# BitLinear feed-forward on one core: left blocks of a pair made two pairs ahead, both int8 roundings of a pair on ScalarE

## The chip, the cores and the metric

One core of one Trainium2 chip runs the whole program. The metric is device time in microseconds (us) for one execution, the median of three runs. The core's engines are TensorE (PE in the rows; PEld is its weight load), VectorE (DVE), ScalarE (ACT), GpSimd (POOL) and SyncE (SP), whose queue issues nearly all DMAs here.

## The reference

8192 tokens (128 x 64) of 256 values go through a conditioned RMS norm, a gated up-projection to 2 x 1024, an exact GELU gate, an int8-style rounding per token, and a down-projection with ternary weights:

```python
scale = cond @ norm_w.T + 1.0
h = x * (scale[:, None, :] * rsqrt(mean(x * x, -1) + 1e-6))
val, gate = split(h @ up_w.T)                 # 256 -> 2 x 1024
h = val * gelu(gate)                          # exact
hq = round(h * 127 / max|h|) * max|h| / 127   # per token
y = hq @ ternary(down_w).T + x                # 1024 -> 256
```

## The kernel before

**Tiles.** Tokens are taken in 64 groups of 128 (`G` = 64), four groups to a tile of x (`NG` = 4). A group's left matrix is h: 128 tokens by 256, and its product with the up weights is made in two chunks (`NJ`) of 512 columns, each with a gate and a value half. fp32 operands are split into a high and a low fp16 part and multiplied as hi x hi, hi x lo, lo x hi.

**Pairs.** Groups 12 to 55 (`W0` to `W1`) run as 22 pairs (`NP`). For a pair, chunk 0 is multiplied group by group (`project`), and chunk 1 by a scheme with seven block products instead of eight, for which sums and differences of the pair's left blocks and of weight blocks are needed. So a pair has two left tiles, each turned (transposed) by one DMA into `hpT`: part 0, the own blocks, and part 1, the sums. `hpT` and `hp_hl` have two buffers each. The way of a left tile is: VectorE multiplies x by its scales (`scale_h` into `hp`, line 821, one instruction for each group); GpSimd makes the four sums (`pair_sums`, lines 409 to 414); ScalarE casts to the high part (`pair_high`, line 568); GpSimd subtracts for the low part (`pair_low`, line 418); SP issues the transposing DMA (`turn_pair`, line 299), which must also wait until TensorE is done with that buffer, two pairs back.

**TensorE's order in a pair** (`pair`, products of three matmuls at lines 1097 to 1099, projections of six at 1084 to 1089): the first chain product; gate of the first group; the down-projection of an older group (`downs`, eight matmuls, line 1221); the second chain product, the first that reads part 1; value of the first group; a product into another bank; the third chain product; a product into the bank `ps_two`; gate of the second group; the fourth chain product; value of the second group; the down-projection of another older group; the last product into `ps_two`. The chain accumulates in one bank, and ScalarE copies it out between its products (`pair_copy` 0, 1, 2; lines 575 and 579): the second chain product waits for copy 0, the third for copy 1, the fourth for copy 2.

**Rounding.** For each group VectorE reduces the maximum over 1024 columns, clips it, inverts it and makes the dequantising scale (`token_scale`, `dequant_scale`, lines 878 to 889). In a pair, the earlier group is rounded to int16 on VectorE (line 901) and cast to bf16 there (906); the other is scaled by `trec127` (line 1023), rounded on ScalarE at the end of its pair (`pair_quantise`, line 601) and cast on VectorE (898). SP turns the bf16 tile (`turn_q`, line 307, into `qT`), TensorE multiplies it (`down`), ScalarE scales the result (`scale_y`, line 626), GpSimd adds x (`sum_y`, line 455), and SP stores four groups at once (312) and loads a later tile of x (269). `quantised(g)` says how many groups are rounded by the step of group g: two fewer than g in the pairs.

**Order.** Each engine's order is written out by hand and an engine takes its instructions in that order; a wait on a semaphore holds everything behind it on that engine's queue. In pair i, whose first group is g = 12 + 2i: VectorE begins with `scale_h` of pair i+1, then finishes pair i-1 (`pair_first`: `pair_add` at line 860, the product at 869), then rounds. GpSimd makes the sums and low parts of pair i+1. SP turns part 0 of pair i+1, turns an older q, stores and loads, turns part 1 of pair i+1, and turns the next q.

Of the kernel before, what the change touches and what calls it, by code (L numbers as in the profile page):

```python
# [5 lines left out]
def cond_bitlinear_ffn(nc: bass.Bass, x, cond_norm, up_wT, down_wT, out):  # L6
# [75 lines left out]
    with ctx:  # L82
# [73 lines left out]
        trec127 = sb("trec127", [P, 1], fp32)  # L156
# [104 lines left out]
        def _(sp):  # L261
# [68 lines left out]
            def loads(g):  # L330
                t, n = g // NG, g % NG
                if n == 2 and t + 2 < NT:
# [50 lines left out]
        def _(pool):  # L383
# [97 lines left out]
            for g in range(F32G, W0):  # L481
                if g + AHEAD < W0:
                    low_part(g + AHEAD)
                elif g + AHEAD == W0:
                    pair_sums(0)
                    pair_low(0, 0)
                else:
                    pair_low(0, 1)
                sum_downed(g)
                next_rms(g)  # L490
                if 4 <= g < 8:
                    weight_sum(g - 4)
                if 7 <= g < 11:
                    weight_sum_low(g - 7)
            for i in range(NP):
                g = W0 + 2 * i
                if i >= 1:
                    pair_second(i - 1)
                if i + 1 < NP:
                    pair_sums(i + 1)  # L500
                    pair_low(i + 1, 0)
                    pair_low(i + 1, 1)
                else:
                    low_part(W1)
                    low_part(W1 + 1)
                sum_downed(g)
                next_rms(g + 1)
                sum_downed(g + 1)
            pair_second(NP - 1)
            for g in range(W1, G + 2):  # L510
# [3 lines left out]
                next_rms(g)  # L514

        @block.scalar
        def _(act):
# [143 lines left out]
            for g in range(F32G, W0):  # L661
# [3 lines left out]
                else:  # L665
                    pair_high(0, g + AHEAD - W0)
# [14 lines left out]
                if g % NG < 2:  # L681
                    squares(g // NG + 1, 2 * (g % NG))
                gelu(NJ * g)
            gelu(NJ * W0 - 1)
            for i in range(NP):
# [4 lines left out]
                if i + 1 < NP:  # L690
                    pair_high(i + 1, 0)
                else:
                    high_part(W1)
                pair_copy(i, 1)
                if i + 1 < NP:
                    pair_high(i + 1, 1)
                else:
                    high_part(W1 + 1)
                pair_gelu(i, 1)
                pair_copy(i, 2)  # L700
                if i == 0:
                    squares(g // NG + 1, 0)
                if g % NG == 0:
                    squares(g // NG + 1, 2)
                else:
                    squares(g // NG + 2, 0)
                pair_gelu(i, 2)
                pair_gelu(i, 3)
                scale_downed(g + 1)
                for n in range(quantised(g), quantised(g + 1)):  # L710
                    pair_quantise(n)
            for g in range(W1, G + 2):
# [5 lines left out]
                if g % NG == 1 or (g % NG == 0 and g > W1):  # L718
                    squares(g // NG + 1, 2 * (g % NG))
# [4 lines left out]
        def _(dve):  # L724
# [266 lines left out]

            for g in range(F32G, W0):
                if g + AHEAD < W0:
                    scale_h(g + AHEAD)
                elif g + AHEAD == W0:
                    scale_h(W0)
                    scale_h(W0 + 1)
# [9 lines left out]
            for i in range(NP):  # L1007
                g = W0 + 2 * i
                scale_h(g + 2)
                scale_h(g + 3)  # L1010
                if i >= 1:
                    pair_first(i - 1)
                quantise_step(g)
                pair_first_chunk(i, 0)
                pair_add(i, 1)
                late = range(quantised(g), quantised(g + 1))
                for n in late:
                    token_scale(n)
                    dequant_scale(n)
                    dve.wait_ge(trec_ready, n + 1)  # L1020
                    if n >= W0:
                        dve.wait_ge(qint_ready, n - 1)
                    nc.vector.tensor_scalar(trec127[:, :], trec[:, n % 2:n % 2 + 1], 127.0, None, ALU.mult)\
                        .then_inc(trec127_ready, 1)
                pair_first_chunk(i, 1)
                for n in late:
                    quantise(n, there=True)
            pair_first(NP - 1)
            for g in range(W1, G):
# [275 lines left out]
```

## Time and profile before

| what | us |
|---|---|
| median of 3 runs | 424.87 (424.78 to 426.2) |
| profiled execution, its time | 423.69 |
| profiled execution, its span | 421.9 |
| TensorE busy (matmuls), share | 394.4, 93% |
| VectorE, ScalarE, GpSimd busy | 340.1, 245.2, 221.4 |
| mean granted clock of TensorE, share of full | 0.982 |

The span runs from the first to the last instruction of the profiled execution; 1.8 us of its time lie around it. Busy time of an engine is an average over stages: the first 82 us are groups 0 to 11, then come the 22 pairs to about 364 us, then the last eight groups. A full clock of TensorE is 2.4 GHz; the other level it shows is half of that.

### The profile page before, as it was taken

How to read it: one execution, taken by the hardware profiler on the slowest of the kernel's cores; microseconds unless marked ns; L12 is line 12 of the kernel's file. 1: busy time of each engine (PE TensorE's matmuls, PEld its weight loads, DVE VectorE, ACT ScalarE, POOL GpSimd, SP SyncE). 2: the span in 40 equal slices, each digit the busy share in tenths (PEclk: the TensorE clock that was granted, in tenths of full speed). 3: DMA queues.
4: the chain of work that ended last, by engine and by line, in shares of the span. 5: the costliest groups of instructions: out<-in, count | busy, mean ns of one | idle time of the engine just before them, and what ended most of it. 6: DMA issues, size and time to landing. Idle time of an engine off the chain costs nothing.

```text
span 421.9 us, 6611 instructions
## 1 busy us (share of the span) xinstructions
PE 394.4 (93%) x2006; PEld 201.8 (48%) x2006; DVE 340.1 (81%) x651; ACT 245.2 (58%) x487; POOL 221.4 (52%) x288
## 2 busy tenths in 40 slices
PE   7999999999996997979979899897998989999996
PEld 4444445555553553534535455354543545455555
DVE  3698998869897795985958979797795988999874
ACT  3565565377675674646746667665764666633322
POOL 2042457567684664744747656675664764323112
PEclk9999999999999998999989999999998999999999
DMA  8165435865929486292691946939385383655433
GB/s 264 65 191 88 110 66 125 193 145 101 212 54 218 66 171 118 50 208 55 137 175 28 213 82 150 155 64 198 77 175 113 63 161 76 127 99 130 82 91 125
DMA packets 132027, 52.96 MB, mean 126 GB/s; under 512 B 123608, under 2 KB 127512, under 8 KB 131992
## 3 DMA queue, kind: packets, MB, share of 16 engines
q1 hardware_dynamic: 131704, 52.28, 59.3%
q8 instruction: 16, 0.26, 0.3%
q10 hardware_dynamic: 288, 0.26, 0.2%
q14 instruction: 19, 0.16, 0.1%
HBM read 13.60 MB, written 8.52 MB: 52 GB/s over the span
## 4 chain that ended last, share of the span: by engine, by line
PE 54%; DMA 14%; DVE 11%; issue 8%; SPq 5%; ACT 4%; POOL 1%; DVEq 0%; ACTq 0%; POOLq 0%
DMA hpT<-hp_hl 14%; PE ps_val L1087 6%; PE ps_val L1084 6%; PE ps_val L1089 6%; PE ps_gate L1089 5%; PE ps_gate L1084 5%; PE ps_gate L1087 5%; PE ps_y L1221 5%; PE ps_gate L1097 3%; PE ps_gate L1099 3%; PE ps_gate L1098 3%; ACT q_int L601 2%; DVE q_bf L906 2%; SPq L307 2%; DVE tmax L878 2%
## 5 line engine op out<-in xcount | busy, mean ns | idle before, releaser
L595 ACT ACTIVATE gel<-ps_gate,comp 128x512 f32<-128x512 f32 x88 | 59.5, 687 | 42.1 <-PE ps_gate L1099 20.2
L878 DVE TENSOR_REDUCE tmax<-act_h 128x1 f32<-128x1024 f32 x63 | 76.0, 1207 | 0.1
L455 POOL TENSOR_TENSOR y_out<-y_sc,x_sb 128x256 f32<-128x256 f32 x63 | 48.2, 768 | 52.6 <-ACT y_sc L626 45.7
L418 POOL TENSOR_TENSOR hp_hl<-hp,hp_hl 128x512 f16<-128x512 f32 x44 | 55.4, 1269 | 24.4 <-ACT hp_hl L568 24.4
L1221 PE MATMUL ps_y<-dw_q,qT 128*128 128x256 bf16 x504 | 64.7, 273 | 0.0
L1221 PEld LDWEIGHTS ps_y<-dw_q,qT 128*128 128x128 bf16 x504 | 49.2, 98 | 18.0 <-ACT y_sc L626 0.4
L848 DVE SCALAR_TENSOR_TENSOR act_h<-ps_val,comp,gel 128x512 f32<-128x512 f32 x44 | 32.9, 747 | 29.3 <-PE ps_val L1089 28.8
L1097 PE MATMUL ps_gate<-wt_hi,hpT 128*128 128x512 f16 x66 | 25.3, 383 | 20.9 <-DMA hpT<-hp_hl 20.9
L400 POOL TENSOR_TENSOR h_hl<-h,h_hl 128x256 f16<-128x256 f32 x18 | 12.8, 711 | 52.8 <-ACT h_hl L533 48.8
L558 ACT ACTIVATE gel<-ps_gate,comp 128x512 f32<-128x512 f32 x36 | 24.6, 683 | 26.5 <-PE ps_gate L1089 26.3
L901 DVE TENSOR_SCALAR q_int<-act_h,trec 128x1024 int16<-128x1024 f32 x42 | 37.7, 897 | 0.1
L1087 PE MATMUL ps_val<-w_lo,hpT 128*128 128x512 f16 x88 | 35.4, 402 | 0.0
L1084 PE MATMUL ps_val<-w_hi,hpT 128*128 128x512 f16 x88 | 35.4, 402 | 0.0
L626 ACT ACTIVATE y_sc<-ps_y,deq 128x256 f32<-128x256 f32 x63 | 29.5, 472 | 8.8 <-PE ps_y L1221 8.8
L1087 PE MATMUL ps_gate<-w_lo,hpT 128*128 128x512 f16 x88 | 33.4, 379 | 0.0
L1084 PE MATMUL ps_gate<-w_hi,hpT 128*128 128x512 f16 x88 | 33.4, 379 | 0.0
L579 ACT ACTIVATE u_two<-ps_gate,comp 128x512 f32<-128x512 f32 x22 | 15.1, 687 | 31.1 <-PE ps_gate L1099 31.1
L841 DVE SCALAR_TENSOR_TENSOR act_h<-ps_val,comp,gel 128x512 f32<-128x512 f32 x35 | 26.0, 746 | 7.6 <-PE ps_val L1089 5.7
L906 DVE CAST q_bf<-q_int 128x1024 bf16<-128x1024 int16 x42 | 27.0, 644 | 4.2
L525 ACT ACTIVATE squares_out<-x_sb 128x256 bf16<-128x256 f32 x64 | 25.7, 405 | 4.7 <-DMA x_sb<-x 4.7
L568 ACT CAST hp_hl<-hp 128x512 f16<-128x512 f32 x44 | 26.8, 609 | 2.4 <-DVE hp L821 2.0
L427 POOL TENSOR_TENSOR act_h<-val_two,gel 128x512 f32<-128x512 f32 x22 | 28.2, 1280 | 0.0
(145 smaller groups left out, 877.1 us busy)
## 6 DMA issues: line engine op xcount, KB each, us to landing
x_sb<-x SPq DMA_DIRECT2D x15, 512.0 KB, 5.8
out<-y_out SPq DMA_DIRECT2D x15, 512.0 KB, 3.9
w_in<-up_wT SPq DMA_DIRECT2D x4, 512.0 KB, 6.7
scale_tok<-scale_dram SPq DMA_DIRECT2D x15, 128.0 KB
dw<-down_wT SPq DMA_DIRECT2D x1, 1024.0 KB, 5.9
qT<-q_bf SPq DMA_TRANSPOSE x63, 3.1
hpT<-hp_hl SPq DMA_TRANSPOSE x44, 3.3
out<-y_out SPq DMA_DIRECT2D x4, 128.0 KB, 2.1
```

Of the source, the lines that this page charges most:

```text
L418: nc.gpsimd.tensor_tensor(hp_hl[:, i % 2, part, 1, :, :], hp[:, i % 2, part, :, :], hp_hl[:, i % 2, part, 0, :, :], ALU.subtract).then_inc ...
L455: nc.gpsimd.tensor_tensor(y_out[:, t % 2, n, :], y_sc[:, g % YS, :], x_sb[:, t % XS, n, :], ALU.add)\
L595: nc.scalar.activation(gel[:, place, :], bank[:, :], ACT.Gelu, scale=comp[:, n % 2, GATE:GATE + 1])\
L848: nc.vector.scalar_tensor_tensor(act_h[:, g % HA, 0, :], ps_val[m][:, :], comp[:, 0, VAL:VAL + 1], gel[:, m, :], ALU.mult, ALU.mult).then_ ...
L878: nc.vector.tensor_reduce(tmax[:, i:i + 1], act_h[:, g % HA, :, :], AX.XY, ALU.max, apply_absolute_value=True).then_inc(tmax_ready, 1)
L901: nc.vector.tensor_scalar(q_int[:, i, :], act_h[:, g % HA, :, :].rearrange("p j c -> p (j c)"), trec[:, i:i + 1], 127.0, ALU.mult, ALU.mul ...
L906: nc.vector.tensor_copy(q_bf[:, i, :], q_int[:, i, :]).then_inc(q_ready, 1)
L1084: nc.tensor.matmul(bank[:, :], parts[:, 0, k, :], w_hi[:, j, s, k, :], start=(k == 0), stop=False)
L1087: nc.tensor.matmul(bank[:, :], parts[:, 0, k, :], w_lo[:, j, s, k, :], start=False, stop=False)
L1089: ins = nc.tensor.matmul(bank[:, :], parts[:, 1, k, :], w_hi[:, j, s, k, :], start=False, stop=(k == KD - 1))
L1097: nc.tensor.matmul(bank[:, :], left[:, 0, :], hi, start=start, stop=False, skip_group_check=not start)
L1221: ins = nc.tensor.matmul(ps_y[g % 2][:, 0:D], qT[:, g % QS, f, :], dw_q[:, f, :], start=(f == 0), stop=(f == NF - 1))
```

## The change

Left tiles are made two pairs ahead instead of one: in pair i VectorE multiplies, GpSimd sums and ScalarE casts for pair i+2, in the middle and at the end of the pair. SP turns both parts of pair i+1 at the begin of pair i, ahead of everything else of that pair. Both groups that are rounded in a pair are rounded on ScalarE: the first between copy 1 and the second GELU, the second at the end. `trec127` gets two columns. VectorE's int16-to-bf16 casts come later: that of the second group in the next pair, behind `pair_first`. SP's turns of q, the loads of scales and the squares move accordingly. The last two groups before the pairs make the left tiles of pairs 0 and 1; the last pair makes those of groups 56 and 57, later in the pair than before.

```diff
 # SP
             for g in range(F32G, W0):
                 if g + AHEAD < W0:
                     turn_h(g + AHEAD)
-                else:
-                    turn_pair(0, g + AHEAD - W0)
+                elif g + 1 == W0:
+                    turn_pair(0, 0)
+                    turn_pair(0, 1)
             for i in range(NP):
                 g = W0 + 2 * i
                 if i + 1 < NP:
                     turn_pair(i + 1, 0)
-                else:
-                    turn_h(W1)
+                    turn_pair(i + 1, 1)
+                if i >= 1:
+                    turn_quantised(g - 1)
+                loads(g)
                 turn_quantised(g)
-                loads(g)
-                if i + 1 < NP:
-                    turn_pair(i + 1, 1)
-                else:
-                    turn_h(W1 + 1)
                 loads(g + 1)
-                turn_quantised(g + 1)
+            turn_h(W1)
+            turn_quantised(W1 - 1)
+            turn_h(W1 + 1)
 # GpSimd
                 if i >= 1:
                     pair_second(i - 1)
-                if i + 1 < NP:
-                    pair_sums(i + 1)
-                    pair_low(i + 1, 0)
-                    pair_low(i + 1, 1)
+                sum_downed(g)
+                if i + 2 < NP:
+                    pair_sums(i + 2)
+                    pair_low(i + 2, 0)
+                    pair_low(i + 2, 1)
...
-                sum_downed(g)
-                next_rms(g + 1)
+                if g % NG == 2 and g // NG + 2 < NT:
+                    rms_of(g // NG + 2)
                 sum_downed(g + 1)
 # ScalarE
             def pair_quantise(g):
-                act.wait_ge(trec127_ready, (g - W0) // 2 + 2)
+                act.wait_ge(trec127_ready, g - W0 + 4)
                 act.wait_ge(q_ready, g - 1)
                 nc.scalar.activation(q_int[:, g % 2, :], act_h[:, g % HA, :, :]..., ACT.Copy,
-                                     scale=trec127[:, 0:1]).then_inc(qint_ready, 1)
+                                     scale=trec127[:, g % 2:g % 2 + 1]).then_inc(qint_ready, 1)
...
                 pair_copy(i, 0)
                 scale_downed(g)
                 pair_gelu(i, 0)
-                if i + 1 < NP:
-                    pair_high(i + 1, 0)
...
                 pair_copy(i, 1)
-                if i + 1 < NP:
-                    pair_high(i + 1, 1)
...
+                for n in range(quantised(g - 1), quantised(g)):
+                    pair_quantise(n)
                 pair_gelu(i, 1)
                 pair_copy(i, 2)
...
+                squares(g // NG + 2, g % NG)
+                if i + 2 < NP:
+                    pair_high(i + 2, 0)
+                elif i + 1 == NP:
+                    high_part(W1)
                 pair_gelu(i, 2)
                 pair_gelu(i, 3)
+                if i + 2 < NP:
+                    pair_high(i + 2, 1)
+                elif i + 1 == NP:
+                    high_part(W1 + 1)
                 scale_downed(g + 1)
                 for n in range(quantised(g), quantised(g + 1)):
                     pair_quantise(n)
 # VectorE
+            def scale_step(g):
+                for n in range(quantised(g - 1), quantised(g)):
+                    token_scale(n)
+                    dequant_scale(n)
+                    dve.wait_ge(trec_ready, n + 1)
+                    dve.wait_ge(qint_ready, n - 1)
+                    nc.vector.tensor_scalar(trec127[:, n % 2:n % 2 + 1], trec[:, n % 2:n % 2 + 1], 127.0, None, ALU.mult)\
+                        .then_inc(trec127_ready, 1)
...
             for i in range(NP):
                 g = W0 + 2 * i
-                scale_h(g + 2)
-                scale_h(g + 3)
                 if i >= 1:
                     pair_first(i - 1)
-                quantise_step(g)
+                    for n in range(quantised(g - 2), quantised(g - 1)):
+                        quantise(n, there=True)
+                scale_step(g)
                 pair_first_chunk(i, 0)
+                for n in range(quantised(g - 1), quantised(g)):
+                    quantise(n, there=True)
+                if i + 2 < NP:
+                    scale_h(g + 4)
+                    scale_h(g + 5)
+                elif i + 1 == NP:
+                    scale_h(W1)
+                    scale_h(W1 + 1)
                 pair_add(i, 1)
...
+                scale_step(g + 1)
                 pair_first_chunk(i, 1)
-                for n in late:
-                    quantise(n, there=True)
             pair_first(NP - 1)
+            for n in range(quantised(W1 - 2), quantised(W1 - 1)):
+                quantise(n, there=True)
```

## Rows read from the trace of the kernel before

**Rows 1.** Head of the profile's page.
```profile
span 421.9 us, 6611 instructions
```
**Rows 2.** Waits of TensorE: us in total, times, longest us.
```profile
PE ps_gate L1097 <- DMA hpT<-hp_hl: 20.9, 9, 3.2
```
**Rows 3.** Timeline, TensorE, pair 0: start us, us, engine, line, out<-in.
```profile
82.15 0.38 PE L1097 MATMUL ps_gate<-w_hi,hpT 128*128 128x512 f16 x1
...
84.09 1.04 PE L1221 MATMUL ps_y<-dw_q,qT 128*128 128x256 bf16 x8
...
90.15 0.38 PE L1097 MATMUL ps_gate<-wt_hi,hpT 128*128 128x512 f16 x1
...
92.96 0.38 PE L1097 MATMUL ps_val<-w_hi,hpT 128*128 128x512 f16 x1
```
**Rows 4.** Same view: last products of pairs 1, 2, 21, and one stalled matmul.
```profile
104.42 0.38 PE L1097 MATMUL ps_val<-w_hi,hpT 128*128 128x512 f16 x1
...
116.84 0.38 PE L1097 MATMUL ps_val<-w_hi,hpT 128*128 128x512 f16 x1
...
215.47 0.38 PE L1097 MATMUL ps_gate<-wt_hi,hpT 128*128 128x512 f16 x1 [2.34 <-DMA hpT<-hp_hl]
...
363.69 0.38 PE L1097 MATMUL ps_val<-w_hi,hpT 128*128 128x512 f16 x1
```
**Rows 5.** Windows: length; PE, PEld, DVE, ACT, POOL busy (x); clock; DMA; GB/s.
```profile
209.50:225.15 15.65, 13.31 (x64) 6.32 (x62) 9.87 (x20) 8.52 (x17) 8.31 (x12) 0.89 0.78 148
...
sum 102.52, PE 94.00 PEld 47.85 DVE 83.71 ACT 65.65 POOL 63.97; mean PE 11.75 PEld 5.98 DVE 10.46 ACT 8.21 POOL 8.00
```
**Rows 6.** Timeline, SP's queue, ahead of the stall at 215.47.
```profile
208.48 0.42 SPq L269 DMA_DIRECT2D x_sb<-x  x1
209.00 1.88 SPq L299 DMA_TRANSPOSE hpT<-hp_hl  x1
```
**Rows 7.** VectorE: source view (min/median/max), timeline, groups by line (busy, mean).
```profile
L898 DVE CAST q_bf<-q_int x22: 427/1000/1246, 93.4 to 363.9; 128x1024 bf16<-128x1024 int16 x22
...
207.09 1.20 DVE L878 TENSOR_REDUCE tmax<-act_h 128x1 f32<-128x1024 f32 x1
...
208.72 0.15 DVE L1023 TENSOR_SCALAR trec<-trec 128x1 f32<-128x1 f32 x1
...
L901 DVE TENSOR_SCALAR q_int<-act_h,trec 128x1024 int16<-128x1024 f32 x18 | 17.3, 959 | 0.0
L821 DVE SCALAR_TENSOR_TENSOR hp<-x_sb,rms_s,scale_tok 128x256 f32<-128x256 f32 x36 | 15.7, 477 | 0.3
L869 DVE TENSOR_TENSOR act_h<-val_one,gel 128x512 f32<-128x512 f32 x18 | 14.4, 800 | 0.6
L860 DVE SCALAR_TENSOR_TENSOR val_one<-ps_val,comp,u_two 128x512 f32<-128x512 f32 x18 | 13.3, 742 | 0.0
```
**Rows 8.** ScalarE, groups by line: busy us, mean ns, idle before.
```profile
L568 ACT CAST hp_hl<-hp 128x512 f16<-128x512 f32 x36 | 21.9, 609 | 0.4 <-POOL hp L414 0.4
L601 ACT ACTIVATE q_int<-act_h,trec 128x1024 int16<-128x1024 f32 x19 | 21.8, 1148 | 2.9 <-DVE trec L1023 2.9
L626 ACT ACTIVATE y_sc<-ps_y,deq 128x256 f32<-128x256 f32 x36 | 17.0, 473 | 0.0
L579 ACT ACTIVATE u_three<-ps_gate,comp 128x512 f32<-128x512 f32 x18 | 12.4, 687 | 0.0
```
**Rows 9.** Timeline, GpSimd: first of the four sums, then two low parts.
```profile
200.63 0.45 POOL L409 TENSOR_TENSOR hp<-hp 128x128 f32<-128x128 f32 x1 [1.41 <-DVE hp L821]
...
202.85 2.72 POOL L418 TENSOR_TENSOR hp_hl<-hp,hp_hl 128x512 f16<-128x512 f32 x2
```
**Rows 10.** Source view, transposes of hpT (L299), then of qT (L307), hT (L290).
```profile
DMA to landing us min/median/max: 3.0/3.3/7.0
...
DMA to landing us min/median/max: 3.0/3.1/7.2
...
DMA to landing us min/median/max: 2.4/2.4/5.3
```

More of the change, by code:

```diff
@@ L155, in cond_bitlinear_ffn @@
         trec = sb("trec", [P, 2], fp32)
-        trec127 = sb("trec127", [P, 1], fp32)
+        trec127 = sb("trec127", [P, 2], fp32)
         deq = sb("deq", [P, DEQ], fp32)
@@ L331, in loads @@
                 t, n = g // NG, g % NG
-                if n == 2 and t + 2 < NT:
+                if n == (0 if paired(g) else 2) and t + 2 < NT:
                     load_scale(t + 2)
@@ L483, in _ @@
                     low_part(g + AHEAD)
-                elif g + AHEAD == W0:
-                    pair_sums(0)
-                    pair_low(0, 0)
-                else:
-                    pair_low(0, 1)
+                else:
+                    pair_sums(g + AHEAD - W0)
+                    pair_low(g + AHEAD - W0, 0)
+                    pair_low(g + AHEAD - W0, 1)
                 sum_downed(g)
@@ L494, in _ @@
                     weight_sum_low(g - 7)
+            rms_of(W0 // NG + 1)
             for i in range(NP):
@@ L498, in _ @@
                     pair_second(i - 1)
-                if i + 1 < NP:
-                    pair_sums(i + 1)
-                    pair_low(i + 1, 0)
-                    pair_low(i + 1, 1)
-                else:
+                sum_downed(g)
[4 more added lines that the diff above has]
+                elif i + 1 == NP:
                     low_part(W1)
                     low_part(W1 + 1)
-                sum_downed(g)
-                next_rms(g + 1)
+                if g % NG == 2 and g // NG + 2 < NT:
+                    rms_of(g // NG + 2)
                 sum_downed(g + 1)
@@ L513, in _ @@
                 sum_downed(g)
-                next_rms(g)
         @block.scalar
@@ L665, in _ @@
                 else:
-                    pair_high(0, g + AHEAD - W0)
+                    pair_high(g + AHEAD - W0, 0)
                 scale_downed(g)
@@ L682, in _ @@
                     squares(g // NG + 1, 2 * (g % NG))
+                elif g + 2 >= W0:
+                    squares(W0 // NG + 1, 2 * (g + 2 - W0))
+                    pair_high(g + 2 - W0, 1)
                 gelu(NJ * g)
@@ L717, in _ @@
                 scale_downed(g)
-                if g % NG == 1 or (g % NG == 0 and g > W1):
-                    squares(g // NG + 1, 2 * (g % NG))
                 if g < G:
@@ L994, in _ @@
                     scale_h(g + AHEAD)
-                elif g + AHEAD == W0:
-                    scale_h(W0)
-                    scale_h(W0 + 1)
+                else:
+                    scale_h(2 * (g + AHEAD) - W0)
+                    scale_h(2 * (g + AHEAD) - W0 + 1)
                 combine(NJ * g - 1)
@@ L1008, in _ @@
                 g = W0 + 2 * i
-                scale_h(g + 2)
-                scale_h(g + 3)
                 if i >= 1:
                     pair_first(i - 1)
-                quantise_step(g)
+                    for n in range(quantised(g - 2), quantised(g - 1)):
+                        quantise(n, there=True)
+                scale_step(g)
                 pair_first_chunk(i, 0)
-                pair_add(i, 1)
-                late = range(quantised(g), quantised(g + 1))
-                for n in late:
[L1018 to L1024, printed above, removed]
+                for n in range(quantised(g - 1), quantised(g)):
[3 more added lines that the diff above has]
+                    scale_h(g + 5)
+                elif i + 1 == NP:
+                    scale_h(W1)
+                    scale_h(W1 + 1)
+                pair_add(i, 1)
+                scale_step(g + 1)
                 pair_first_chunk(i, 1)
-                for n in late:
-                    quantise(n, there=True)
             pair_first(NP - 1)
+            for n in range(quantised(W1 - 2), quantised(W1 - 1)):
+                quantise(n, there=True)
             for g in range(W1, G):
```

10 lines of the change are left out of this document (removed).

## The prediction

> **What bounds the kernel now.** I read the page's head first [rows 1]: the span is 421.9 us, and the profiled execution took 423.69. Then the waits of TensorE, the busiest engine: in the whole run it has one wait that matters, 20.9 us in 9 waits for a transposed left tile, always before the second chain product [rows 2]. Then its timeline, to get the length of a pair. Pair 0 starts at 82.15 and its last product at 92.96 [rows 3]; the last product of pair 1 starts at 104.42 [rows 4]. So a pair without a stall takes 104.42 - 92.96 = 11.46 us, and in it TensorE has no gap. Pair 2 ends 12.42 later, at 116.84, but it holds a third group of down-projections (the lag of `downed` changes from 5 to 4 at group 16), so that is work. From there to pair 21's last product at 363.69 [rows 4] there are 19 pairs in 246.85 us; at 11.46 they would be 217.74. **29.1 us are lost in the pairs.** 20.9 are the waits. Most of the rest is TensorE's clock: the stretch with the stall of 2.34 us before 215.47 [rows 4] has a granted clock of 0.89 over 15.65 us [rows 5], so 1.7 us at the half level of 1.2 GHz after that stall; the stretch is 4.19 longer than a clean pair, 2.34 of it the wait and 1.7 the clock.
>
> Why the tile is late is seen in SP's queue: in every second pair the turn of part 1 is issued at 209.00, right behind a load of x at 208.48 (and a store before it) [rows 6], and TensorE starts on it at 215.47, 6.5 us after the issue, near the slowest landing of 7.0; the median is 3.3 [rows 10].
>
> **The change part by part.** Times below count from the start of a pair.
>
> *The left tiles.* `turn_pair` waits for TensorE's end of the pair before, as buffers demand, and now comes first in SP's order. Both issues are then done by 0.2 + 2 x 1.9 = 4.0 at an issue of 1.88 [rows 6], and landed by 4.0 + 7.0 = 11.0 at the slowest landing [rows 10], ahead of the next pair's start at 11.46 and its second chain product. So all of the 20.9 goes, and with it the clock's drops, since the clock falls after these stalls. The blocks themselves are made a pair earlier; what they cost on VectorE, GpSimd and ScalarE stays the same and only changes place. Gain: 29.1 us.
>
> *VectorE and ScalarE.* For each pair one int16 rounding of 0.96 leaves VectorE and one of 1.15 joins ScalarE, and one scaling of 0.15 is added on VectorE [rows 7, 8]. Means of eight pairs are 10.46 busy on VectorE, 8.21 on ScalarE and 8.00 on GpSimd [rows 5], so afterwards about 9.65, 9.36 and 8.0 of 11.46. None becomes the bound by its sum alone. What is left is order, so I follow two chains.
>
> *First chain, to TensorE.* The new rounding stands in ScalarE's order ahead of the second GELU and of copy 2, and the fourth chain product waits for copy 2. From the end of the pair before (results about 0.2 into the pair): `pair_add` 0.74, product 0.80, cast 0.43 to 1.25, the step from maximum to `trec127` 208.72 + 0.15 - 207.09 = 1.78 [rows 7], rounding 1.15, copy 0.69 [rows 8] and the GELU, which reads as many columns, at the copy's price. The sum is 6.5 to 7.3; some 0.3 for handovers between engines is my estimate (the rounding on ScalarE follows its `trec127` within hundredths). The fourth chain product has its place at 90.15 - 82.15 = 8.0 [rows 3]. So 0.4 to 1.2 us of slack: no cost on the path, though thin.
>
> *Second chain, around all engines.* ScalarE's last rounding of a pair releases a cast on VectorE (0.43 to 1.25), then 1.78 to `trec127`, 1.15 rounding, another cast 0.43 to 1.25, two multiplications 0.95, GpSimd's sums 202.85 - 200.63 = 2.22, ScalarE's high part 0.61, its scaling of y 0.47, and the last rounding 1.15 [rows 7 to 9]. That is 9.2 to 10.8, with handovers 9.5 to 11.1. Below 11.46, so it turns inside a pair; it costs nothing, and up to 0.2 us a pair were the casts both slow and the handovers twice my estimate.
>
> A rule speaks against this. A cast alone takes 0.43, and up to 1.25 beside GpSimd's work [rows 7]. The Trainium skill, "SBUF — State Buffer", section "Who interferes with whom", says that a VectorE cast in its fast mode and a GpSimd instruction exclude one another, and that the later one waits for the whole of the other. By that a cast could take a whole low part more; by the row it took at most 1.25. I keep the row for the sum and give the other case as a rival.
>
> *The turns of q.* They are moved behind both tile turns and partly behind store and load. The first of a pair, cast at 1.7 + 0.43 to 1.25 = 2.2 to 3.0, is issued at about 4.0 and lands at 7.1 by the median [rows 10]; its down-projection starts about one group of eight (1.04) before the last product at 92.96 - 82.15 = 10.8 [rows 3], so near 9.8. The second is cast at 5.5 to 7.2 (rounded at 3.95 to 4.8 plus 1.15) and lands 3.1 to 7.2 later [rows 10], 8.6 to 14.4; it is wanted by the next pair's first down-projection at 11.46 + 84.09 - 82.15 = 13.4 [rows 3]. At the median there are 3 us to spare; at the slowest landing, which falls on turns behind a load, it is 1.0 late. Cost 0 to 1.0 in each of some 10 pairs with a load; I take 0.
>
> *Entry and handover.* The last two groups before the pairs get two multiplications more on VectorE, 0.95 [rows 7]; its products there wait for TensorE, so I take 0.3 of 0 to 1.0. In the last pair the left tile of group 56 is multiplied only after the second cast, so from about 6.1 to 7.2: one multiplication 0.48, a high part of at most 0.61, a low part of at most 2.72 / 2 = 1.36 [rows 9], landing 2.4 to 5.3 [rows 10], altogether 10.9 to 15. Its place is 11.46. Cost 0 to 3.5 plus 1.7 of clock; near the lower end (small tile, no load of x left), 0.3.
>
> *Sum.* 423.69 - 29.1 + 0.3 + 0.3 + 1.0 for small waits that such thin slack will show somewhere (chosen, 0.05 a pair) = 396.2 for a profiled execution. The median of the runs lies 1.2 above the profiled one (424.87 against 423.69), so the forecast is **397.4 us**.
>
> **The rivals.** *Casts wait for GpSimd.* If each cast waits for a whole low part (2.72 / 2 = 1.36 [rows 9]), it takes 1.36 + 0.43 = 1.8 instead of 1.25 and the second chain becomes 11.1 + 2 x 0.55 = 12.2 a pair. 22 x (12.2 - 11.46) = 16 more: about 413. For it: the casts now stand beside GpSimd's low parts of two pairs ahead. Against: GpSimd is busy 8.0 in a pair [rows 5], so the two casts will not both meet the begin of one of its longest instructions. This is the rival that the skill's page gives.
>
> *A q is late.* The second turn lands behind store and load, 0.5 to 1.0 us too late in 10 pairs: 5 to 10 more, 402 to 407. For it: slowest landing [rows 10]. Against: SP issues that turn some 2 us after the load, where before the tile's turn came 0.5 after it [rows 6].
>
> *Slower.* ScalarE takes its rounding in order, so GELU and copy 2 are held until `trec127` is there. Each microsecond by which the first chain passes 8.0 is a microsecond a pair. It eats the gain at 8.0 + 29.1/22 = 9.3; at 10.0, say with VectorE's whole step of the pair before still ahead of it, a pair takes 13.5, and 22 x 2.0 = 44 - 29 gives 15 more than now, 440. Against: the sum of 6.5 to 7.3 would have to be wrong by 2.
>
> *It does not do what it says.* The turns of both parts are first in the queue but still wait, for low parts that GpSimd makes late in the pair before. Were these later than 4 us into the pair, the stall would stay, and the time with it, near 424. Against: 8.0 busy on GpSimd leave it 3.4 a pair to catch up.
>
> **How the numbers follow.** Forecast 0.73 (395 to 400); casts wait 0.08; q late 0.10; slower 0.05; no effect 0.04. The low end, 394.5, is the whole gain without any cost (424.87 - 29.1 = 395.8) and the scatter of runs; the high end, 408, takes in the late q and small waits of 0.5 a pair. Beyond it lie the waiting casts, no effect and slower, 0.17. A measurement of this kernel can tell about 0.5% from no change, 2 us: faster 0.91, within 0.04, slower 0.05.
>
> **What would show it.** In the profile after: no wait of TensorE for hpT; pairs of 11.46 from one last product to the next; a granted clock of 1.0 in the pairs; the turns of both parts issued within 4 us of a pair's start; ScalarE's two roundings of 1.15 per pair, the first starting near 4.5; VectorE busy about 9.7 in a pair. The forecast is wrong if TensorE waits at the fourth chain product for a copy (first chain), if its down-projection waits for qT (q late), if pairs are evenly longer than 11.46 with casts near 1.8 (casts wait), or if the last eight groups begin with a gap of over 1 us.

## The result, and the profile after

| | before | after |
|---|---|---|
| median of 4 runs, us | 424.82 | 400.74 (398.17 to 402.38) |
| profiled execution, us | 423.69 | 401.6 |
| mean granted clock | 0.982 | 0.996 |

The changed kernel takes 0.943 of the time of the one before (95% interval 0.9365 to 0.9496). The forecast was 397.4 with a range of 394.5 to 408. In the experiments below some executions of the kernel before are slow ones, and the ratios to it leave those out.

The head of the page after, and TensorE's waits there (us in total, times, longest); the rows answer to [rows 1] and [rows 2]:

```profile
span 399.7 us, 6678 instructions
```

```profile
PE ps_gate L1105 <- ACT gel L595: 3.7, 1, 3.7
...
PE ps_gate L1092 <- DMA hT<-h_hl: 0.8, 1, 0.8
...
PE ps_y L1229 <- ACT y_sc L626: 0.4, 1, 0.4
```

The nine waits for `hpT` are gone. In their place stand three single waits that the kernel before did not have. Where they are is read from the timeline of TensorE: the last products of pairs 0, 1, 2 and 21, the first matmuls of pair 1, and a down-projection in pair 2 (start us, us):

```profile
93.31 0.38 PE L1105 MATMUL ps_val<-w_hi,hpT 128*128 128x512 f16 x1
...
97.81 0.58 PE L1105 MATMUL ps_gate<-w_hi,hpT 128*128 128x512 f16 x1 [3.69 <-ACT gel L595]
...
99.05 0.63 PE L1092 MATMUL ps_gate<-w_hi,hpT 128*128 128x512 f16 x1
99.47 0.63 PE L1095 MATMUL ps_gate<-w_lo,hpT 128*128 128x512 f16 x1
...
109.94 0.38 PE L1105 MATMUL ps_val<-w_hi,hpT 128*128 128x512 f16 x1
...
121.99 1.05 PE L1229 MATMUL ps_y<-dw_q,qT 128*128 128x256 bf16 x8 [0.43 <-ACT y_sc L626]
122.87 0.38 PE L1105 MATMUL ps_val<-w_hi,hpT 128*128 128x512 f16 x1
...
340.60 0.38 PE L1105 MATMUL ps_val<-w_hi,hpT 128*128 128x512 f16 x1
```

From pair 2 to pair 21 there are 340.60 - 122.87 = 217.73 us for 19 pairs: 11.46 each, and nothing is lost. Before, the same stretch took 246.85 [rows 4]. But pair 1 ends 16.63 after pair 0, which is 5.17 too late: a gap of 3.69, and behind it matmuls that start 0.42 apart instead of 0.22, TensorE at its half level (the last section has the window: 1.4 us lost in it). Of the four executions only this one shows the half level: its mean granted clock is 0.996, that of the three others (398.17 to 402.38) 1.0. Pair 2 is 0.6 too late as well (12.93, of which 0.87 is its third down-projection): that is the wait of 0.43 at 121.99 for `y_sc` and what a stop costs beside its wait (0.15 to 0.16, the last section). It has nothing to do with the gap, since the runs of the changed kernel below that have no gap keep it.

Why TensorE waits at pair 1 is seen on ScalarE, in order of time in pair 0 (copy 2, then the squares of x tile 5, then two GELUs):

```profile
88.76 0.69 ACT L579 ACTIVATE u_three<-ps_gate,comp 128x512 f32<-128x512 f32 x1
95.10 0.42 ACT L525 ACTIVATE squares_out<-x_sb 128x256 bf16<-128x256 f32 x1 [5.65 <-DMA x_sb<-x]
...
96.42 1.25 ACT L595 ACTIVATE gel<-ps_gate,comp 128x512 f32<-128x512 f32 x2
```

and in SP's queue, where the load they wait for is issued at 91.09, behind another load of x, two turns and a load of scales:

```profile
85.96 0.42 SPq L269 DMA_DIRECT2D x_sb<-x  x1
86.42 3.97 SPq L299 DMA_TRANSPOSE hpT<-hp_hl  x2
...
91.09 0.46 SPq L269 DMA_DIRECT2D x_sb<-x  x1
```

The change moves the squares of tile 5 from pair 1 into pair 0, and tile 5's load is issued only in pair 0. It happens once: later tiles are loaded some three pairs ahead.

The other pairs look as in these windows (length; busy of PE, PEld, DVE, ACT, POOL with counts; clock; DMA share; GB/s), two of eight and their mean, which answers to [rows 5]:

```profile
139.74:151.20 11.46, 11.46 (x63) 5.97 (x62) 9.60 (x20) 8.83 (x17) 6.89 (x9) 1.00 0.49 99
151.20:162.66 11.46, 11.46 (x63) 5.98 (x62) 9.18 (x21) 9.43 (x18) 8.25 (x11) 1.00 0.91 190
...
sum 91.68, PE 91.68 PEld 47.74 DVE 75.10 ACT 73.07 POOL 60.55; mean PE 11.46 PEld 5.97 DVE 9.39 ACT 9.13 POOL 7.57
```

TensorE fills all of them, at full clock. VectorE has fallen from 10.46 to 9.39 and ScalarE risen from 8.21 to 9.13 (before, in stretches of 12.8 us on the mean, stalls included).

### The profile page after: what moved, and what is told of

Read it like the earlier page. It is cut to its first block, busy times and chain, and to the rows that moved or that the text cites. A ratio compares the mean times of both kernels' runs of the same rounds, so it can differ in the third digit from the quotient of the medians.

```text
span 399.7 us, 6678 instructions
## 1 busy us (share of the span) xinstructions
PE 388.3 (97%) x2006; PEld 201.1 (50%) x2006; DVE 319.3 (80%) x651; ACT 265.8 (67%) x509; POOL 213.1 (53%) x288
## 4 chain that ended last, share of the span: by engine, by line
PE 89%; DVE 3%; DMA 2%; POOL 2%; SPq 1%; issue 1%; ACT 1%; DVEq 0%; ACTq 0%
PE ps_y L1229 12%; PE ps_gate L1092 8%; PE ps_gate L1095 8%; PE ps_gate L1097 8%; PE ps_val L1097 8%; PE ps_val L1092 8%; PE ps_val L1095 8%; PE ps_gate L1105 6%; PE ps_gate L1107 6%; PE ps_gate L1106 6%; PE ps_gate L1081 2%; PE ps_val L1107 2%; PE ps_val L1106 2%; PE ps_val L1105 2%; PE ps_val L1081 2%
## 5 line engine op out<-in xcount | busy, mean ns | idle before, releaser
L595 ACT ACTIVATE gel<-ps_gate,comp 128x512 f32<-128x512 f32 x88 | 58.7, 685 | 13.3 <-PE ps_gate L1097 9.9
L455 POOL TENSOR_TENSOR y_out<-y_sc,x_sb 128x256 f32<-128x256 f32 x63 | 51.6, 821 | 25.9 <-ACT y_sc L626 19.0
L418 POOL TENSOR_TENSOR hp_hl<-hp,hp_hl 128x512 f16<-128x512 f32 x44 | 51.4, 1180 | 5.8 <-ACT hp_hl L568 5.8
L601 ACT ACTIVATE q_int<-act_h,trec 128x1024 int16<-128x1024 f32 x44 | 50.6, 1149 | 5.4 <-DVE trec L997 5.4
L409 POOL TENSOR_TENSOR hp<-hp 128x128 f32<-128x128 f32 x22 | 10.0, 456 | 76.5 <-DVE hp L819 76.5
L400 POOL TENSOR_TENSOR h_hl<-h,h_hl 128x256 f16<-128x256 f32 x18 | 12.8, 711 | 56.0 <-ACT h_hl L533 52.0
L558 ACT ACTIVATE gel<-ps_gate,comp 128x512 f32<-128x512 f32 x36 | 24.4, 683 | 22.9 <-PE ps_gate L1097 22.9
L1095 PE MATMUL ps_val<-w_lo,hpT 128*128 128x512 f16 x88 | 33.4, 379 | 0.0
L1092 PE MATMUL ps_val<-w_hi,hpT 128*128 128x512 f16 x88 | 33.4, 379 | 0.0
L896 DVE CAST q_bf<-q_int 128x1024 bf16<-128x1024 int16 x44 | 30.1, 684 | 3.1 <-ACT q_int L601 3.1
L427 POOL TENSOR_TENSOR act_h<-val_two,gel 128x512 f32<-128x512 f32 x22 | 30.3, 1379 | 0.0
L858 DVE SCALAR_TENSOR_TENSOR val_one<-ps_val,comp,u_two 128x512 f32<-128x512 f32 x22 | 16.5, 750 | 15.0 <-PE ps_val L1107 15.0
```

Of the source, the lines that this page charges most:

```text
L418: nc.gpsimd.tensor_tensor(hp_hl[:, i % 2, part, 1, :, :], hp[:, i % 2, part, :, :], hp_hl[:, i % 2, part, 0, :, :], ALU.subtract).then_inc ...
L455: nc.gpsimd.tensor_tensor(y_out[:, t % 2, n, :], y_sc[:, g % YS, :], x_sb[:, t % XS, n, :], ALU.add)\
L595: nc.scalar.activation(gel[:, place, :], bank[:, :], ACT.Gelu, scale=comp[:, n % 2, GATE:GATE + 1])\
L1092: nc.tensor.matmul(bank[:, :], parts[:, 0, k, :], w_hi[:, j, s, k, :], start=(k == 0), stop=False)
L1095: nc.tensor.matmul(bank[:, :], parts[:, 0, k, :], w_lo[:, j, s, k, :], start=False, stop=False)
```

## Experiments

Theory after the result: the gain is the turns' place in SP's queue, ahead of the loads; what was lost against the forecast is the load of x tile 5. Rivals: the lead of two pairs or VectorE's relief brings the gain, and the entry gap has another cause. All times are medians of four runs. Four kernels ran beside one another on one chip: the early load alone, the early turn added to it, SP's order alone, and the changed kernel with the rounding back on VectorE. The others ran in three more groups, on other chips. The kernel before was run in each group, and its executions spread from 418.6 to 434.3, those of most kernels without the stall by 1 to 3 us, so the comparisons below are among the medians of the latter. None of these was run in two groups, so a difference of 1 or 2 us between groups shows little by itself; there the waits in the traces decide.

**The load of x tile 5, issued early.**

```diff
-                if n == 0 and t + 2 < XS:
+                if n == 0 and t + 2 < XS - 1:
                     load_x(t + 2)
+                if g == 8:
+                    load_x(XS - 1)
```

> The changed kernel, with one DMA moved: the load of x tile 5 is issued at group 8, beside that of tile 4, instead of in pair 0 behind two stores or loads and two turns. Theory: ScalarE's squares of tile 5, moved by the change from pair 1 into pair 0, wait 5.65 us for this load, two GELUs stand behind them, and TensorE waits 3.69 us for these and then runs 3.4 us at the half clock (1.6 us). Then this kernel is 5.3 us faster than the changed one's profiled 401.6, so 395.5 to 397, TensorE starts pair 1 without a gap, and its runs scatter less. Rival: the gap at pair 1 comes from the late start of the left tiles at the entry or from VectorE, and the load is only the last of several equal waits: then the gap stays above 2 us and the time is 399 to 401.

396.06 (395.18 to 397.34), ratio to the kernel before 0.9399 (0.931 to 0.9488). ScalarE's squares start right behind copy 2, without a wait (timeline of ScalarE):

```profile
88.05 0.69 ACT L581 ACTIVATE u_three<-ps_gate,comp 128x512 f32<-128x512 f32 x1
88.63 0.41 ACT L527 ACTIVATE squares_out<-x_sb 128x256 bf16<-128x256 f32 x1
```

and TensorE's gap at pair 1 is gone, with the half clock (mean granted clock 1.0). The profiled execution is 5.5 us shorter; 5.3 was expected. So the entry gap is this load.

**The turn of group 57 ahead of an older q, too.**

```diff
             turn_h(W1)
-            turn_quantised(W1 - 1)
             turn_h(W1 + 1)
+            turn_quantised(W1 - 1)
```

> As the run with the early load of x tile 5, and after the pairs SP turns the left tile of group 57 ahead of the q of group 52 instead of behind it. Theory: the wait of 0.80 us for that tile at 348.25 is the queue behind the cast of q 52; without it 0.6 to 0.9 us less than the run with the early load alone, so 395 to 396.4. Rival: the wait only moves to the turn of q 52 and its down-projection, or to VectorE: then no difference (under 0.3).

395.19 (394.49 to 396.01), 0.9 less than the run before it, and the wait of 0.8 for `hT` is no longer among TensorE's waits. The two kernels' runs overlap a little, so the time alone would not show it; the wait that went does.

**SP's order alone, in the kernel before.**

```diff
                 turn_quantised(g)
-                loads(g)
                 if i + 1 < NP:
                     turn_pair(i + 1, 1)
                 else:
                     turn_h(W1 + 1)
+                loads(g)
                 loads(g + 1)
```

> The kernel before, with SP's queue alone changed: in a pair the store and the loads of x and of scales are issued after the turn of part 1 instead of ahead of it. Left tiles are still made one pair ahead, the first rounding stays on VectorE. Theory A: the stall was the turn's place behind 1.1 MB of loads alone; the turn is then issued near 8.5 us into the pair and lands by 12, wanted at 14.3: TensorE has no wait for hpT, and the time is 396 to 400. Theory B: with pairs of 11.46 VectorE at 10.46 busy falls behind, the low parts come later from pair to pair and the waits come back in part: 403 to 412. No effect: above 420.

394.42 (394.33 to 396.78), ratio 0.9371 (0.9274 to 0.9468): no wait for `hpT`, as theory A has it, a time below its 396 to 400, and all of the gain, with one line moved and no lead of two pairs. SP's queue in a pair with loads now reads as follows (start us, us):

```profile
193.22 1.37 SPq L307 DMA_TRANSPOSE qT<-q_bf  x1
194.69 1.26 SPq L299 DMA_TRANSPOSE hpT<-hp_hl  x1
196.01 0.61 SPq L283 DMA_DIRECT2D scale_tok<-scale_dram  x1
196.67 0.47 SPq L312 DMA_DIRECT2D out<-y_out  x1
197.18 0.42 SPq L269 DMA_DIRECT2D x_sb<-x  x1
```

where [rows 6] had the load ahead of the turn. The move takes away two delays at once: some 1.6 us in which SP issued the three loads ahead of the turn, and part of the landing, whose slowest falls from 7.0 [rows 10] to 5.0 (source view). This run does not part them. The last products of pairs 0 and 21 lie 241.59 apart, 21 pairs of 11.46 and one more down-projection:

```profile
92.75 0.38 PE L1097 MATMUL ps_val<-w_hi,hpT 128*128 128x512 f16 x1
...
334.34 0.38 PE L1097 MATMUL ps_val<-w_hi,hpT 128*128 128x512 f16 x1
```

VectorE does keep up, but with little left (mean of eight pairs):

```profile
sum 91.67, PE 91.67 PEld 47.76 DVE 85.58 ACT 66.13 POOL 66.39; mean PE 11.46 PEld 5.97 DVE 10.70 ACT 8.27 POOL 8.30
```

**How much of the load must go behind the turn.** The same kernel before, with only the load of x moved (`x_loads`); `loads(g, False)` issues the scales and the store, which stay ahead.

```diff
                 turn_quantised(g)
-                loads(g)
+                loads(g, False)
                 if i + 1 < NP:
                     turn_pair(i + 1, 1)
...
+                x_loads(g)
                 loads(g + 1)
```

> The kernel before, with the load of x alone moved behind the turn of part 1; the store of 512 KB and the load of scales stay ahead of it. Theory A: the turn's late landing is the bytes ahead of it, and half of them go: the landing falls from 6.5 to about 4 and nearly all of the stall of 1.4 to 3.2 us goes: 395 to 400. Theory B: one transfer of 512 KB ahead is enough for a stall of 1 us and more in 9 pairs: 405 to 412.

402.03 (401.81 to 406.65): between the two theories, and the slowest landing of a turn is still 6.5. TensorE still waits for `hpT`:

```profile
PE ps_gate L1103 <- DMA hpT<-hp_hl: 6.4, 6, 1.9
```

against 20.9 in 9 [rows 2]. So most of the stall came from the load of x, and the store of 512 KB with the 128 KB of scales ahead of the turn is enough for up to 1.9 us.

**The lead of two pairs without the turns' place.** The changed kernel with both repairs (the early load and the early turn of group 57), and the loads put back between the two turns.

```diff
                     turn_pair(i + 1, 0)
-                    turn_pair(i + 1, 1)
                 if i >= 1:
                     turn_quantised(g - 1)
                 loads(g)
+                if i + 1 < NP:
+                    turn_pair(i + 1, 1)
                 turn_quantised(g)
```

> The changed kernel with the early load of x tile 5 and the early turn of group 57, and in the pairs the store and the loads put back between the two turns of a pair, as in the kernel before: part 0, an older q, store and loads, part 1. Left tiles are still made two pairs ahead. Theory A: the lead alone also removes the stall, since part 1 is issued near 5 us into the pair and, landing 7 later at the worst, is there 2 us before it is wanted at 14.3: same time as without this edit, 394.5 to 396.5, no wait for hpT. Theory B: only the queue's order counts: waits for hpT of 1 to 2.5 us in some 10 pairs come back, 408 or more.

396.09 (395.42 to 398.0): theory A. TensorE has no wait for `hpT`, though the slowest landing is as slow as before (source view of the turns, min/median/max):

```profile
DMA to landing us min/median/max: 3.0/3.5/6.8
```

So either remedy is enough: the turn ahead of the loads, or a lead that outlasts the loads. The rounding of the first group is still on ScalarE here; whether the lead would be enough with VectorE as full as before is not shown.

**The rounding back on VectorE.** In the changed kernel, and then in the changed kernel with both repairs:

```diff
-                act.wait_ge(trec127_ready, g - W0 + 4)
+                act.wait_ge(trec127_ready, (g - W0) // 2 + 2)
...
                 pair_copy(i, 1)
-                for n in range(quantised(g - 1), quantised(g)):
-                    pair_quantise(n)
...
-                scale_step(g)
+                quantise_step(g)
                 pair_first_chunk(i, 0)
-                for n in range(quantised(g - 1), quantised(g)):
-                    quantise(n, there=True)
```

> The changed kernel with the rounding of a pair's first group put back on VectorE (int16 rounding and cast right behind its maximum); left tiles two pairs ahead and SP's order as in the changed kernel. Theory A: the order of the turns gives the whole gain, VectorE at about 10.2 of 11.46 still keeps up: same time as the changed kernel within 1 us, pairs of 11.46. Theory B: VectorE needs the relief: waits of TensorE at the fourth chain product or the value products, pairs of 11.8 to 12.5, 408 to 424.

402.89 (402.5 to 403.26), 2.2 above the changed kernel: outside what theory A expected. But the waits put most of it at the entry, not in the pairs:

```profile
PE ps_gate L1101 <- ACT gel L595: 4.5, 1, 4.5
...
PE ps_y L1225 <- DMA qT<-q_bf: 0.2, 1, 0.2
```

That gap is 0.8 longer than the changed kernel's, mostly because pair 0 ends 0.6 earlier while the load of x lands as late as there; pair 1 begins only 0.25 later, at 98.06. Behind the gap the clock took 2.3 us instead of 1.4 (windows in the last section), so the last product of pair 1 starts 1.24 later, at 111.18 against 109.94:

```profile
111.18 0.38 PE L1101 MATMUL ps_val<-w_hi,hpT 128*128 128x512 f16 x1
```

The one wait for `qT` makes a later pair 0.4 longer. Together that is the 1.7 between the two profiled executions, 403.26 and 401.6. This left open whether the rounding matters at all, so the same edit was made without the entry gap:

> The changed kernel with the early load of x tile 5 and the early turn of group 57 (395.2), and the rounding of a pair's first group put back on VectorE. With the change's late load the same edit gave 402.9, with a gap of 4.5 us at pair 1 and 6.8 us at the half clock. Theory A: that gap was the entry's, not VectorE's, so with the early load this kernel is within 1 us of 395.2. Theory B: the rounding on VectorE itself costs, here too 2 us: 397 to 398, with waits of TensorE inside the pairs.

394.97 (394.29 to 395.7): theory A, and no wait of TensorE for `qT`. Put on ScalarE or left on VectorE, the rounding makes no difference to the time that these runs show.

**What the relief buys.** VectorE burdened with one more maximum over 1024 columns at the end of its pair, once in the kernel before with the loads last, once in the changed kernel with both repairs.

```diff
+            dve.wait_ge(dw_loaded, 16)
...
                 for n in late:
                     quantise(n, there=True)
+                nc.vector.tensor_reduce(burden[:, :], dw[:, 0:4, :], AX.XY, ALU.max, ...)
...
                 pair_first_chunk(i, 1)
+                nc.vector.tensor_reduce(burden[:, :], dw[:, 0:4, :], AX.XY, ALU.max, ...)
```

> The kernel before with the loads behind both turns (394.4), and VectorE burdened with one more maximum over 1024 columns (1.2 us, its result unused) at the end of each pair. It was busy 10.70 of 11.46 there. Theory: with 11.9 VectorE becomes the bound and each pair grows by about 0.5: 403 to 408. Rival: waits for TensorE that VectorE has in a pair hide it: 394.5 to 397.

> The changed kernel with the early load of x tile 5 and the early turn of group 57 (395.2), and VectorE burdened with the same maximum (1.2 us) at the same place, the end of its pair. It was busy 9.44 of 11.46. Theory: 10.7 fits; 0.7 of the burden lies in VectorE's wait for TensorE at the pair's end, the other 0.5 goes into the first chain, whose slack in the trace is 0.7 to 1.05: no cost, 394.5 to 396.5. Rival: the first chain is thinner than that, TensorE waits at the fourth chain product: 399 to 406.

403.83 (403.42 to 404.7) and 396.82 (395.86 to 397.3). The first is 9.4 above its kernel without the burden: with 10.70 of 11.46 used, 1.2 more does not fit, and its pairs last 11.7 to 12.2 instead of 11.46. TensorE waits for the copies (PEld is its weight load, where these waits show; they lie partly beside matmuls and sum to more than the time lost):

```profile
PEld ps_gate L1100 <- ACT u_two L580: 10.3, 15, 0.9
PEld ps_gate L1100 <- ACT u_three L580: 6.2, 14, 0.5
```

The second is 1.6 above its own: not quite free, since in five pairs, 0.1 to 0.4 us longer than the others, the weight load waits for copy 2, but the burden fits. The change bought VectorE room that this kernel does not use.

**How thick the first chain's slack is.** ScalarE burdened between the first rounding and the second GELU with a copy of 512 or 1024 columns, in the changed kernel with both repairs.

```diff
                     pair_quantise(n)
+                nc.scalar.copy(burden[:, :, :], dw[:, 0:2, :])     # 0:4 for 1024 columns
                 pair_gelu(i, 1)
```

> The same changed kernel (395.2), and ScalarE burdened with a copy of 512 columns (about 0.58 us from start to start, its result unused) between the first rounding and the second GELU. In the trace copy 2 ends 6.95 to 7.24 into the pair and is wanted at 8.0. Theory: 0.58 fits into the first chain's slack of 0.75 to 1.05: no cost, 394.5 to 397. Rival: the slack is used up elsewhere (ScalarE's last rounding of the pair comes late for the next pair): 400 or more.

> The changed kernel with the early load of x tile 5 and the early turn of group 57 (395.2), and ScalarE burdened with a copy of 1024 columns (about 1.06 us from start to start, its result unused) between the first rounding and the second GELU. Theory: the first chain's slack is 0.75 in every second pair and 1.05 in the others, so copy 2 comes 0.3 late in about 10 pairs and just in time in the others: 3 to 5 us more, 398 to 401, with TensorE waiting for copy 2 at the fourth chain product. Rivals: no cost, under 397 (slack over 1.1 in all pairs); or ScalarE as a whole is the bound, over 404.

395.34 (394.48 to 395.87): 512 columns cost nothing that shows. 401.82 (401.22 to 404.01): 1024 columns cost 6.6, in every second pair, at the place foretold:

```profile
PE ps_gate L1109 <- ACT u_three L582: 4.2, 10, 0.5
```

```profile
219.78 0.59 PE L1101 MATMUL ps_gate<-w_hi,hpT 128*128 128x512 f16 x2
220.81 0.39 PE L1109 MATMUL ps_gate<-wt_hi,hpT 128*128 128x512 f16 x1 [0.44 <-ACT u_three L582]
```

A stop costs more than its wait: after two matmuls from 219.78 the next would have started 2 x 0.216 later, at 220.21, and it starts at 220.81, 0.60 late for a wait of 0.44. Ten such stops make 4.2 + 10 x 0.16 = 5.8 of the 6.6; a wait for `y_sc` of 0.8 instead of 0.4 and one of 0.3 for `hT` are the rest. Expected were 3 to 5. In nine of the ten pairs that stop, the first chain is longer than the trace without a burden showed, because one VectorE step in it takes 1.71 or 1.72 instead of 1.34 (the product, line 867 of the changed kernel, 871 here; the last section says why). In the pair of the stall at 220.81:

```profile
213.20 1.71 DVE L871 TENSOR_TENSOR act_h<-val_one,gel 128x512 f32<-128x512 f32 x1
```

## Why the prediction was right, point by point

**The bound and the gain.** Right: pairs of 11.46 and 29.1 us lost in them. All of it came back from pair 2 on. The 8.2 us beside the waits are mostly the clock, as was said, but the clock fell after four of the nine stalls only: 6.8 us in these four, and 1.4 are what nine stops cost beside their waits (the last section).

**The left tiles.** Right that the turns, first in the queue, are in time. But the cause, the turn's place behind the load, was named there without drawing the consequence: putting it ahead of the loads is enough (394.42), and neither the lead nor the rounding on ScalarE adds to it.

**First chain.** Worked out as 6.5 to 7.3 us with 0.3 for handovers, wanted at 8.0. The changed kernel's timelines, ScalarE's rounding and copy 2 in two pairs,

```profile
197.21 1.15 ACT L601 ACTIVATE q_int<-act_h,trec 128x1024 int16<-128x1024 f32 x1 [0.58 <-DVE trec L997]
...
198.83 0.68 ACT L579 ACTIVATE u_three<-ps_gate,comp 128x512 f32<-128x512 f32 x1
...
209.99 0.69 ACT L579 ACTIVATE u_three<-ps_gate,comp 128x512 f32<-128x512 f32 x1
```

and TensorE's first and fourth chain product,

```profile
192.28 0.38 PE L1105 MATMUL ps_gate<-w_hi,hpT 128*128 128x512 f16 x1
...
200.27 0.38 PE L1105 MATMUL ps_gate<-wt_hi,hpT 128*128 128x512 f16 x1
...
211.73 0.38 PE L1105 MATMUL ps_gate<-wt_hi,hpT 128*128 128x512 f16 x1
```

have copy 2 end 199.51 - 192.28 = 7.23 into one pair and 6.94 into the next (210.68, pair start 203.74), wanted at 7.99. The slack of 0.4 to 1.2 was right, and the burdens confirm it: 0.58 fits, 1.06 does not. One term was mis-sized: in every second pair the product takes 1.34 instead of 0.80. The sum still holds, since its upper end has a cast of 1.25, and the cast there takes 0.94 to 0.95.

**Second chain, turns of q, busy times.** No wait of TensorE for a cast or for `qT` in the pairs of the changed kernel; the slowest landing of `qT` is 5.9. VectorE, ScalarE and GpSimd are busy 9.39, 9.13 and 7.57 in a pair, foretold as 9.65, 9.36 and 8.0.

**Entry: the term that was mis-sized.** It was set at 0.3 for two multiplications on VectorE, of 0 to 1.0. Measured: 0.35 by the end of pair 0 (93.31 against 92.96 [rows 3]; among the runs of this document that point lies anywhere from 92.2 to 93.3, so this shows no cost of the multiplications), then 5.17 in pair 1, 5.5 in all. The step that failed is that the squares, moved a pair earlier, were passed over as "move accordingly": the load that they wait for and the place where it is issued are in no term of the sum.

**Handover.** 0.3 against 0.9 (one wait of 0.80). The tile that came late was not group 56's, which the prediction followed, but 57's, queued behind a q that waits for a late cast.

**Small waits.** 1.0 against 0.5: pair 2 takes 12.93 where it took 12.42 before, by the one wait for `y_sc`. The sum by the measured terms is 394.6 + 5.5 + 0.9 + 0.5 = 401.5, and the profiled execution took 401.6.

**From one execution to the median.** Here luck helped. The forecast added 1.2 because the median before lay that much above the profiled execution; after, it lies 0.9 below it (400.74 against 401.6). So the profiled execution is 5.4 above its forecast of 396.2, and the median only 3.3 above 397.4. It lies inside the stated range, but not between 395 and 400, where the forecast put 0.73 of its chance.

**The rivals.** None came about as a whole. In the changed kernel no q was late; in two of the later runs (the early load alone, and the first with the rounding back on VectorE) one was, by 0.2. Slower, or no effect, were far off. The mechanism of "Casts wait for GpSimd" is real, but half of the casts meet no GpSimd instruction and most others take 0.95, not 1.8, so it cost no time: see the last section.

## What to carry to other kernels

When TensorE waits for a small DMA, look first at what stands ahead of it in its queue: moving half a megabyte or more of stores and loads behind it took one line here and gave as much as rebuilding four engines' order. When work is moved earlier, list the loads that it waits for and where each is issued, at the entry above all, where a steady state's lead does not hold yet. Before judging relief of an engine, ask whether it was the bound: it brings no time until it is, only room, and a burden put on it measures how much.

## What the runs showed of the hardware that was not expected

**Casts and one product on VectorE, when they meet a running GpSimd instruction, end a fixed time after it.** In the changed kernel (source view, min/median/max) the product of two SBUF tiles and the casts read:

```profile
L867 DVE TENSOR_TENSOR act_h<-val_one,gel x22: 691/693/1431, 98.6 to 342.2; 128x512 f32<-128x512 f32 x22
```

```profile
L896 DVE CAST q_bf<-q_int x44: 415/428/1485, 88.2 to 342.8; 128x1024 bf16<-128x1024 int16 x44
```

In the kernel before, the product took at most 0.81 and the casts at most 1.25. What makes the difference is what GpSimd (POOL) runs when they start. A cast of the kernel before and a product of the changed one, each with the GpSimd instruction that it meets (start us, us):

```profile
198.25 1.25 DVE L898 CAST q_bf<-q_int 128x1024 bf16<-128x1024 int16 x1
```

```profile
197.95 1.27 POOL L427 TENSOR_TENSOR act_h<-val_two,gel 128x512 f32<-128x512 f32 x1
```

```profile
216.18 1.36 DVE L867 TENSOR_TENSOR act_h<-val_one,gel 128x512 f32<-128x512 f32 x1
```

```profile
215.71 1.28 POOL L427 TENSOR_TENSOR act_h<-val_two,gel 128x512 f32<-128x512 f32 x1
```

The cast ends at 199.50, 0.28 after GpSimd's 199.22; the product at 217.54, 0.55 after 216.99. So it is throughout the two traces: each of the 33 casts of q before and 24 after that start beside a running GpSimd instruction with more than 0.15 left ends 0.28 to 0.29 behind it, and the others take 0.41 to 0.43. The product ends 0.55 behind a GpSimd product, sum or low part, and takes 0.69 when it meets none of these. VectorE's maxima over 1024 columns take 1.21 beside GpSimd as well as alone. Before, it met the end of a sum in 20 of 22 pairs, with 0.25 left: 0.80. After, in every second pair, it mostly meets GpSimd's product, with about 0.80 left: 1.35. With 1024 more columns on ScalarE 1.16 are left there: 1.71. The Trainium skill, "SBUF — State Buffer", section "Who interferes with whom", says that a VectorE instruction with two SBUF inputs contends with a GpSimd instruction that reads SBUF, the later one waiting. The rows agree; beside GpSimd's root of the RMS, which reads four columns, the product is not longer than alone. The prediction had applied the rule to casts only, and had set the row's 1.25 against it. But the two are not rivals: 1.25 was the rule with 0.96 left, and in the changed kernel one cast found 1.20 left and took 1.49. It cost no time, because the first chain has the slack.

**The half clock after a gap is not the same each time.** Windows right behind a gap (length; busy of PE, PEld, DVE, ACT, POOL with counts; granted clock; DMA share; GB/s). In the changed kernel, after the gap of 3.69:

```profile
97.81:101.23 3.42, 3.42 (x11) 1.34 (x12) 3.39 (x5) 2.66 (x5) 2.98 (x3) 0.60 0.57 111
```

With the rounding back on VectorE, after the gap of 4.5:

```profile
98.06:104.90 6.84, 6.84 (x25) 3.13 (x26) 5.69 (x10) 4.03 (x7) 4.38 (x4) 0.66 0.60 115
```

And in the kernel before, after a stall of 3.17, after the one of 2.34 [rows 4], and a whole pair with a stall of 2.44:

```profile
135.09:138.50 3.41, 3.41 (x16) 1.56 (x17) 0.77 (x2) 1.75 (x3) 1.29 (x2) 1.00 0.85 163
215.47:218.90 3.43, 3.43 (x9) 1.25 (x10) 0.71 (x2) 1.19 (x2) 0.96 (x1) 0.55 0.93 112
...
286.50:300.56 14.06, 11.62 (x63) 5.91 (x61) 9.87 (x20) 8.52 (x17) 8.31 (x12) 1.00 0.90 162
```

The length times what the clock lacks of 1.00 is lost: 3.42 x 0.40 = 1.4, 6.84 x 0.34 = 2.3, nothing, and 3.43 x 0.45 = 1.5. By whole pairs, from one last product to the next, the nine stalled pairs of the kernel before are of two kinds. Beyond 11.46 and the wait, five have 0.15 to 0.16 more (waits of 3.17, 2.44, 1.92, 1.81 and 1.36), the price of the stop itself, and four have 1.84 to 1.85 more (2.85, 2.58, 2.47 and 2.34), so about 1.7 of clock. The longest stall cost no clock and one of 2.34 did, so the length of a gap alone doesn't tell its price: it was the gap, 0.15 to 0.16, and 0 to 2.3 us of clock.
